# Table reads packed on VectorE, the order of stores and loads on SyncE, and TensorE's set number kept in registers, in the routed stage of a Mamba and mixture-of-experts kernel

## The reference

```
x = x + tanh(g_xattn) * mamba(context, layernorm(x))
h = layernorm(x), 2048 tokens of 512 values
scores = softmax(h @ gate_w.T)                      # 16 experts
weights, ids = top_k(scores, 6), weights normalised to sum 1
out = sum over the six experts e: weight_e * (silu(g) * u) @ w2[e].T, with g, u = split(h @ w13[e].T)   # 352 each
out = out + shared swiglu of width 704, on all tokens
x = x + tanh(g_ffn) * out
```

## Time and profile before

| | |
|---|---|
| median of 3 runs | 1445.77 us (1439.89 to 1447.3) |
| profiled execution | 1442.46 us, span 1440.7 us |
| granted TensorE clock, mean | 0.968 |
| PE, PEld busy | 1321.2 us (92%), 1172.1 us (81%) |
| POOL, DVE, ACT busy | 948.1 us (66%), 853.9 us (59%), 731.9 us (51%) |
| DMA queues q0, q1, q10, share of 16 engines | 23.7%, 23.6%, 7.8% |

### The profile page before, as it was taken

The page is one execution under the profiler, slowest core; times in us unless marked ns, Lnnn a source line. Parts: engine busy times, 40 slices in busy tenths (PEclk is TensorE's granted clock), DMA queues, the critical chain, the costliest instruction groups (busy, mean ns, idle before and its releaser), DMA issues.

```text
span 1440.7 us, 31551 instructions
## 1 busy us (share of the span) xinstructions
PE 1321.2 (92%) x8064; PEld 1172.1 (81%) x8065; DVE 853.9 (59%) x1469; ACT 731.9 (51%) x1317; POOL 948.1 (66%) x671
## 2 busy tenths in 40 slices
PE   7897998998898899999889999999999999999995
PEld 3686887888888799999778878888888888788885
DVE  6878898888999854653344444444444444444442
ACT  5898897898889363333223333333332333333321
POOL 0588899998898657886446645566636665646632
PEclk8899999997999999999999999999999999999998
DMA  4121113221252554564677777888787777877862
GB/s 137 41 72 30 56 64 109 62 99 56 75 166 68 144 123 91 144 151 71 178 174 207 199 212 173 202 208 211 198 182 194 218 195 206 213 183 195 209 165 36
DMA packets 136276, 205.91 MB, mean 143 GB/s; under 512 B 20496, under 2 KB 74384, under 8 KB 134016
## 3 DMA queue, kind: packets, MB, share of 16 engines
q0 software_dynamic: 31024, 62.10, 23.7%
q1 hardware_dynamic: 101744, 102.33, 23.6%
q10 hardware_dynamic: 3440, 40.63, 7.8%
HBM read 130.99 MB, written 76.25 MB: 144 GB/s over the span
## 4 chain that ended last, share of the span: by engine, by line
PE 36%; DMA 14%; issue 7%; DVE 4%; DVEq 4%; POOL 3%; ACT 1%; POOLq 1%; ACTq 0%; SPq 0%
PE bank L1777 11%; PE bank L1757 10%; PE bank L1758 10%; DMA xs<-token_quarters 6%; DMA token_quarters<-xt 4%; DMA xt<-token_rows,gid 3%; PE bank L1768 2%; POOL w L1033 2%; DVEq L1435 2%; DVEq L1429 1%; DVE hs L1223 1%; PE bank L1667 1%; PE bank L1653 1%; ACT ah L908 1%; DVE xl L1423 1%
## 5 line engine op out<-in xcount | busy, mean ns | idle before, releaser
L1757 PE MATMUL bank<-w,xh 128*128 (+1 forms) x1088 | 370.3, 341 | 27.5 <-DVE am L1453 14.7
L995 POOL TENSOR_TENSOR hc<-hs,crow 128x512 f32<-128x512 f32 x254 | 322.0, 1299 | 89.0 <-DVE hs L1223 83.4
L1061 POOL DMA_INDIRECT out_x<-ys,aid x104 | 170.4, 1638 | 277.0 <-issue 234.3
L1758 PE MATMUL bank<-w,xh 128*128 (+1 forms) x1088 | 351.5, 324 | 0.0
L1223 DVE TENSOR_TENSOR_SCAN hs<-dA,bank 128x512 f32<-128x512 f32 x256 | 295.8, 1208 | 50.3 <-PE bank L1667 32.4
L1777 PE MATMUL bank<-w,ah 128*128 (+1 forms) x816 | 262.6, 403 | 20.3 <-DVE al L1459 19.8
L1757 PEld LDWEIGHTS bank<-w,xh 128*128 128x128 f32 x1088 | 204.9, 188 | 60.6 <-issue 56.8
L914 ACT COPY ys<-bank 128x512 f32<-128x512 f32 x136 | 79.8, 586 | 259.6 <-PE bank L1777 259.6
L1758 PEld LDWEIGHTS bank<-w,xh 128*128 128x128 f32 x1088 | 206.9, 190 | 2.3
L1777 PEld LDWEIGHTS bank<-w,ah 128*128 128x128 f32 x816 | 150.5, 190 | 52.5 <-issue 27.2
L1758 PE MATMUL bank<-w,xl 128*128 (+1 forms) x544 | 175.9, 323 | 0.0
(11 more groups left out here) (184 smaller groups left out, 1996.8 us busy)
## 6 DMA issues: line engine op xcount, KB each, us to landing
raws<-in_wall ACTq DMA_DIRECT2D x16, 2176.0 KB, 9.0
token_quarters<-xt SPq DMA_DIRECT2D x104, 256.0 KB, 4.3
xs<-token_quarters SPq DMA_DIRECT2D x104, 256.0 KB, 3.7
crow<-c_rows SPq DMA_DIRECT2D x64, 256.0 KB, 3.2
xt<-token_rows_turned SPq DMA_DIRECT2D x32, 256.0 KB, 3.1
out_x<-ys POOLq DMA_DIRECT2D x32, 256.0 KB, 4.1
token_rows<-rowb SPq DMA_DIRECT2D x4, 1028.0 KB, 6.1
xrow<-in_x SPq DMA_DIRECT2D x4, 1024.0 KB, 8.0
```

The source lines that it names most:

```text
L995: nc.gpsimd.tensor_tensor(hc[:, j, :], hs[:, j, :], crow[:, n % 4, :], ALU.mult).then_inc(hc_done, 1)
L1061: pool.indirect_dma_start(out_rows, bass.IndirectOffsetOnAxis(ap=aid[:, s:s + 1], axis=0), ys[:, s, :], None, bounds_check=TOKENS - 1, oob ...
L1757: nc.tensor.matmul(gate_bank[:, 0:I], xx, columns(w, off + ww + k * 2 * I, I), start=first, stop=last)
L1758: mm = nc.tensor.matmul(up_bank[:, 0:I], xx, columns(w, off + ww + k * 2 * I + I, I), start=first, stop=last)
```

## The change

The unused row 1 of the table now holds three numbers in one word (the next set to prepare, the number of tile t+1's set, and the column of tile t+5), and DVE reads that once a tile and takes it apart by remainder and quotients (`packed` is a new scratch tile for building the word; `sloti` and `odd` go). The ids for the add are copied from `gid` and not from `lists`, for tile t+1 and not t, ahead of `gather_ids`; so they wait for the add of tile t-3. SP stores tile t+1 ahead of the load of tile t (the first store stands ahead of the loop, the last three loads behind it). PE reads the next tile's number in the fourth tile of a round too, and keeps number and offset in two registers over the rounds.

```
@@ -661,10 +660,14 @@
                 for b in range(G):
                     sp.dma_start(gw[b * Q:(b + 1) * Q], gateT[b * P:(b + 1) * P].rearrange("(a c) e -> c a e", c=Q)).then_inc(gw_in, 16)
 
-            def move(t, s, m):
+            def put_quarters(t, s, m=None):
 
                 rows_in(sp, t, s, m, "sp")
+                apart(sp, xt_turned, t - 3, "sp")
                 sp.dma_start(quarters_d[s].rearrange("a p j -> p a j"), xt[:, s, 0:H].rearrange("p (a j) -> p a j", a=G)).then_inc(put[s], 16)
+
+            def set_quarters(t, s, m=None):
+
                 of_slot(sp, put[s], t, m, "sp")
                 apart(sp, xt_turned, t - 3, "sp")
                 sp.dma_start(xs[:, s, :], quarters_d[s].rearrange("a (r g) j -> (a r) (g j)", g=G)).then_inc(moved[s], 16)
@@ -693,10 +696,17 @@
             for t in range(20, NS):
                 x_load(t)
             sp.wait_ge(meta_ready, 2)
-            groups = routed_groups(sp)
-            with sp.Fori(0, groups) as i:
+            looped = sp.value_load(fours[0:1, 2:3], min_val=E // 4 - 2, max_val=ROUTED // 4 - 2)
+            put_quarters(NS, 0)
+            with sp.Fori(0, looped + 1) as i:
                 for k in range(4):
-                    move(4 * i + NS + k, k, i)
+                    put_quarters(4 * i + NS + k + 1, (k + 1) % 4, i + (k + 1) // 4)
+                    set_quarters(4 * i + NS + k, k, i)
+            rest = tiles_but_12(sp) + 8
+            for k in range(3):
+                put_quarters(rest + k + 1, k + 1, looped + 1)
+                set_quarters(rest + k, k, looped + 1)
+            set_quarters(rest + 3, 3, looped + 1)
             tiles = tiles_but_12(sp) + 12
             for s in range(4):
                 apart(sp, added[s], 4 * tiles, "sp")
@@ -1396,9 +1406,6 @@
                 if half == 0:
                     chained(nc.vector.tensor_tensor(slot[:], slot[:], tileno[:, 1, :], ALU.add))
                     chained(nc.vector.tensor_scalar(meta[:, 0, :], slot[:], 1.0, None, ALU.add))
-                    chained(nc.vector.tensor_copy(sloti[:], slot[:]))
-                    chained(nc.vector.tensor_scalar(odd[:], sloti[:], 1, None, ALU.bitwise_and))
-                    chained(nc.vector.tensor_scalar(meta[:, 1, :], odd[:], float(2 * WCOLS), None, ALU.mult))
                     return
                 chained(nc.vector.memset(fresh[:, 0:1], 0.0))
                 chained(nc.vector.tensor_tensor(fresh[:, 1:NT], slot[:, 1:NT], slot[:, 0:NT - 1], ALU.subtract))
@@ -1408,6 +1415,12 @@
                                                        op0=ALU.is_lt, op1=ALU.mult))
                 nc.vector.scalar_tensor_tensor(out=meta[:, 2, :], in0=slot[:], scalar=1.0, in1=fresh[:],
                                                op0=ALU.add, op1=ALU.mult).then_inc(meta_ready, 1)
+                dve.wait_ge(meta_ready, 2)
+                n = NT - AHEAD
+                chained(nc.vector.scalar_tensor_tensor(out=packed[:, 0:n], in0=meta[:, 0, 1:n + 1], scalar=float(NX), in1=meta[:, 2, 0:n],
+                                                       op0=ALU.mult, op1=ALU.add))
+                chained(nc.vector.scalar_tensor_tensor(out=meta[:, 1, 0:n], in0=meta[:, 4, AHEAD:NT], scalar=float(NX * (NX + 1)),
+                                                       in1=packed[:, 0:n], op0=ALU.mult, op1=ALU.add))
 
             def turn(t, s4, m=None):
 
@@ -1422,25 +1435,28 @@
                 source = xt[:, t % 4, 0:H] if isinstance(t, int) and t < NS else banks[4 + 2 * s][:]
                 nc.vector.tensor_tensor(xl[:, s, :], source, xh[:, s, :], ALU.subtract).then_inc(xl_done, 1)
 
-            def take_weight(t, s4, m=None):
-
-                if isinstance(t, int) and t < NS:
-                    return
-                e = dve.value_load(meta[0:1, 0, bass.ds(t, 1)], min_val=1, max_val=NX)
+            def plan_of(t):
+
+                word = dve.value_load(meta[0:1, 1, bass.ds(t, 1)], min_val=0, max_val=NX * (NX + 1) * NR - 1)
+                return dve.snap(word % NX), dve.snap(word // NX % (NX + 1)), dve.snap(word // (NX * (NX + 1)))
+
+            def take_weight(t, s4, number, m=None):
+
                 rows_in(dve, t, s4, m, "dve")
                 at_least(dve, am_done, t - 1)
-                nc.vector.tensor_copy(cc[:, s4 % 2:s4 % 2 + 1], xt[:, s4, bass.ds(H - 1 + e, 1)]).then_inc(cc_done, 1)
+                nc.vector.tensor_copy(cc[:, s4 % 2:s4 % 2 + 1], xt[:, s4, bass.ds(H - 1 + number, 1)]).then_inc(cc_done, 1)
 
             def ids_column(t):
                 return dve.value_load(meta[0:1, 4, bass.ds(t, 1)], min_val=0, max_val=NR - 1)
 
-            def gather_ids(t, s4):
-                nc.vector.tensor_copy(gid[:, s4:s4 + 1], lists[:, bass.ds(ids_column(t), 1)]).then_inc(gid_done, 1)
+            def gather_ids(t, s4, column=None):
+                nc.vector.tensor_copy(gid[:, s4:s4 + 1], lists[:, bass.ds(ids_column(t) if column is None else column, 1)]).then_inc(gid_done, 1)
 
             def add_ids(t, s4):
 
+                apart(dve, gid_done, t + 1, "dve")
                 apart(dve, added[s4], through(t - 4, s4), "dve")
-                nc.vector.tensor_copy(aid[:, s4:s4 + 1], lists[:, bass.ds(ids_column(t), 1)]).then_inc(aid_done, 1)
+                nc.vector.tensor_copy(aid[:, s4:s4 + 1], gid[:, s4:s4 + 1]).then_inc(aid_done, 1)
 
             def multiply(t, s):
                 dve.wait_ge(sg_done, t + 1)
@@ -1468,9 +1484,8 @@
                 if k == EARLY - 1:
                     low.then_inc(wl_done, 1)
 
-            def next_weights(t):
-
-                e = dve.value_load(meta[0:1, 2, bass.ds(t, 1)], min_val=0, max_val=NX - 1)
+            def next_weights(t, e):
+
                 with dve.If(e > 0):
                     apart(dve, raw_in, raws_of(e), "dve")
                     apart(dve, down_done, t, "dve")
@@ -1506,24 +1521,31 @@
                     else:
                         fill_table(i)
 
-            def tile(t, s4, gathers=False, adds=False, m=None):
-                s = s4 % 2
-                if not (isinstance(t, int) and t + 1 < NS):
-                    turn(t + 1, (s4 + 1) % 4, m)
-                a_low(t - 1, 1 - s)
-                take_weight(t + 1, (s4 + 1) % 4, m)
-                if isinstance(t, int):
+            def tile(t, s4, gathers=False, m=None):
+                s, after = s4 % 2, (s4 + 1) % 4
+                if isinstance(t, int) and t < PEELED:
+                    a_low(t - 1, 1 - s)
                     beside(DVE_AFTER_A, t)
-                if isinstance(t, int) and t < NS:
                     for late in FIRST_ROWS.get(t, ()):
                         gather_ids(late, late % 4)
-                elif gathers:
-                    gather_ids(t + AHEAD, (s4 + 1) % 4)
+                    x_low(t + 1, 1 - s)
+                    multiply(t, s)
+                    return
+                split, number, column = plan_of(t)
+                turn(t + 1, after, m)
+                a_low(t - 1, 1 - s)
+                take_weight(t + 1, after, number, m)
+                add_ids(t + 1, after)
+                if gathers:
+                    apart(dve, aid_done, t + 2, "dve")
+                    gather_ids(t + AHEAD, after, column)
+                else:
+                    for late in FIRST_ROWS[t]:
+                        apart(dve, aid_done, t + 2, "dve")
+                        gather_ids(late, late % 4)
                 x_low(t + 1, 1 - s)
-                if adds:
-                    add_ids(t, s4)
                 multiply(t, s)
-
+                next_weights(t, split)
 
             dve.sem_inc(cc_done, NS)
             dve.sem_inc(xt_turned, NS)
@@ -1552,18 +1574,13 @@
             groups = routed_groups(dve)
 
             tile(PEELED, PEELED % 4)
-            next_weights(PEELED)
             for k in range(1, 4):
-                tile(PEELED + k, (PEELED + k) % 4, True, True)
-                next_weights(PEELED + k)
+                tile(PEELED + k, (PEELED + k) % 4, True)
             with dve.Fori(0, groups - 1) as i:
                 for k in range(4):
-                    t = 4 * i + NS + 3 + k
-                    tile(t, (3 + k) % 4, True, True, i + 1)
-                    next_weights(t)
+                    tile(4 * i + NS + 3 + k, (3 + k) % 4, True, i + 1)
             last = tiles_but_12(dve) + 11
             a_low(last - 1, 0)
-            add_ids(last, 3)
             multiply(last, 1)
             a_low(last, 1)
 
@@ -1814,14 +1831,19 @@
                 beside(PE_AFTER_DOWN, t)
             pe.wait_ge(meta_ready, 2)
             groups = routed_groups(pe)
+            carried, carried_old = pe.alloc_register("carried"), pe.alloc_register("carried_old")
+            pe.reg_mov(carried, 2)
+            pe.reg_mov(carried_old, 2 * WCOLS)
             with pe.Fori(0, groups) as i:
-                number = set_number(4 * i + PEELED)
-                old = offset_of(set_number(4 * i + PEELED - 1))
```

(11 more changed lines are left out.)

## The result

| kernel | median us (lowest to highest) | profiled execution, span |
|---|---|---|
| before, beside it | 1446.47 (1439.89 to 1447.3) | 1442.46, 1440.7 |
| after | 1469.16 (1466.95 to 1474.47) | 1467.74, 1466.0 |

The ratio is 1.0172, 95% interval 1.0131 to 1.0214. The change costs some 25 us; the forecast was 8. The direction was right and the size was not.

A forecast was written before the change was run, and what follows sets the result against it. PE was taken as the bound whenever fed. Windows and queueing 14 to 23 us less about 10 outside gave +4 to +13, taken as +8: 1450.5 profiled, 1454 against the median; range 1424 to 1470, the forecast's own 1449 to 1459.

The forecast's parts named there:

- TensorE's registers: PE's table reads at the heads of rounds go; worth 19.7 us where nothing else is late.
- VectorE's table: Three of DVE's four reads go, removing most of 6.8 us `xl` wait; added remainder and quotients cost at most 0.5 us, hidden.
- the ids' wait: DVE's ids copy waits for the add of t-3, delaying tile Q-1 at an expert; nothing added, since Q is later still.
- Outside the windows: The 27 tiles outside the fifteen five-tile windows (Q-4 to Q) give back 12 us, 2.6 only moving a window's start.
- SyncE's order at an expert: Load Q stands behind gather Q+1, the first gather behind the split: windows +14 us, up to +9 for queueing behind a store.
- What a late transpose costs: From DVE's late transpose to the start of its tile on PE: 3.5 us.
- The mechanism forecast: At an expert load Q waits for the delayed gather Q+1, so Q starts late; fifteen windows grow from 522 to 536 us.
- A: Faster rival: load Q lands in 2.6 us, giving 1432; 1407 if gather Q+1's wait did not matter; chance 0.36 with its parts.
- B: Slower rival: load Q served wholly behind the store, 6.0 us instead of 4.1, giving 1482; chance 0.14.
- C: Rival: quotients in registers cost far more than the rows say, deciding from 2 us a tile; chance 0.04.
- Idle ahead of down risen to some 50: Sign at experts: PE idle ahead of "down" rises from 17.6 to some 50 us, DVE's transpose of Q awaiting its load.
- Load Q issued 0.4 us behind store: Sign that the steps are right: at each expert SyncE issues load Q 0.4 us behind store Q+1.

The follow-up runs named there:

- e3: The kernel before with TensorE's carried registers alone: 1425.63 us, ratio 0.9899.
- e4: The kernel before with VectorE's part alone (one packed read, ids copied from `gid` for tile t+1): 1443.28 us, ratio 1.0005.
- e6: The changed kernel with the weights' fetch cut to an eighth, splits reading resident weights, so products are of other weights: 1460.32 us, ratio 1.0121.
- e9: The changed kernel with GpSimd's low split in two halves, one in each of two tiles, the add and gather Q+1 between: 1468.34 us, ratio 1.0185.
- e14: e9 with the weights' fetch in four DMAs, one in each of four tiles, ScalarE carrying the numbers in registers: 1422.24 us, ratio 0.9853.
- e16: e9 with the whole fetch issued at once as two DMAs, in pieces of 1,088 bytes instead of 17,408: 1427.79 us, ratio 0.9868.
- e17: e3 with the whole fetch issued at once as two DMAs in pieces of 1,088 bytes: 1424.66 us, ratio 0.9865.
- e13: e3 with the fetch in four DMAs, one in each of four tiles, and three more table reads on ScalarE per tile: 1551.91 us, ratio 1.0741.
- e5: The changed kernel with SyncE's wait for gather t+1 kept ahead of load t, but store t+1 issued behind that load: 1455.17 us, ratio 1.0074.

## Why the prediction was wrong in size

- **TensorE's registers, 19.7 us: right.** Alone they gave 15 to 18 (e3).
- **VectorE's table: right as to the quotients, wrong as to `xl`.** The three numbers are taken out of the word on the lines that use them, in register operations of 180, 107 and 60 ns at the median (after, L1447, L1453, L1489); before, the two of these lines that had any took 64 and 53 (L1432, L1438). That is 0.23 us more a tile, inside the 0.5 us. But the reads' gain on `xl` was eaten by the ids' wait, to which I had given nothing (e4: 0 us; `xl` wait 14.5 against 6.8). In the changed kernel that error costs nothing: there DVE waits 13.1 us ahead of the ids, none of it for an add, since tile Q-3 is late first. With the fetch out of the way it does cost (e6: DVE waits 46.6 us, PE 26.3).
- **Outside the windows, 12 us less 2.6: right.** Measured 14.3.
- **SyncE's order at an expert, +14 to +23: the step that failed.** It read: "In an even stretch that costs nothing, since the transpose waits long after the landing", and it put the order's whole cost on the load of Q, with the 4 to 5 us seen there. The windows gave +38.5, of which tile Q-3 alone +56.8 and tile Q -15.9. No stall stands ahead of tile Q: Q-1 takes 6.69 us on the mean where it took 6.70. The order took 3.7 us of slack from load Q-2, which is now issued behind the fetch at fifteen experts instead of five, and takes 10 us there. I had the minimum and median of the loads but passed over their maximum, 8.9, though that row was on the page, and no term priced what a load beside a fetch takes: the wait that the sum put at nothing, that of an even stretch, is the one that cost. e9 (no late gather: no change), e14 and e16 (fetch in quarters or short packets: 46 and 40 us less) show it.
- **What a late transpose costs, 3.5 us: too little.** That was read from a short stall. Behind 13 of the 19 stalls PE's clock went to its lower level, and "down" took up to 1.9 us more; some 14 us in all over before.
- **The mechanism forecast exists** (e6: tile Q-1 takes 9.10 us where it took 6.70; the windows are 553.8 instead of the 536 worked out, since the ids' wait is in them too), but in the changed kernel it is behind another stall. I added up costs where the larger hides the smaller, and had the wrong one of the two.
- **Rivals.** A did not come: two windows of fifteen were shorter (39.5 to 37.6 us and 37.1 to 36.9), thirteen longer. The rule of the Trainium skill named there ("DMA: Bandwidth & Descriptors", "Queues, rings and completion order") held, though: in after no load landed before the store issued ahead of it, the nearest 0.40 us behind, while in e5, with the load ahead, the loads landed before the stores. B, a load served wholly behind the store, is right as to the order at load Q-2, whose packets moved behind the store's; its price is not, since the median of the loads in the view is 3.7 us and not 6. C did not come. That 1469.16 lies inside the outer range of 1424 to 1470 is luck: its upper part was B's, and no term of the forecast reached it.
- **What would show it.** "Idle ahead of down risen to some 50": 64.2, but by the transpose of Q-2 and not of Q, so this sign came true for another reason. "Load Q issued 0.4 us behind store": 0.55. "Tiles outside at 6.3 to 6.45": 6.34.

## What to carry to other kernels

Before a transfer is issued later, look at what else the queues carry at its new time and price it with the slowest transfer that the trace shows there (8.9 us here), not the median (3.7); and where several things may be late at one place, take the largest and ask which comes first, since taking away one shows nothing while the other stands. A bulk transfer in rows of 17 KB held the small ones beside it back for as long as it ran. Cutting its rows gave 40 us where a load stood right behind it (e16 against e9), and 1 to 5 us where most did not (e17 against e3). Work on a sequencer between two short instructions of a chain (0.69 us for a read with its branch) cost some 1.2 us a tile in e13 against e3.

## What the runs showed of the hardware that was not expected

- In two stretches beside the fetch two DMA queues moved packets one for one, although these differed 34 and 8.5 times in length: 114 of 17,408 bytes beside 112 of half a KB in 6 us (after), 48 beside 50 of 2 KB in 3 us (e5). At the other experts the small ones got from 0.4 to 1.2 for one (after).
- The same 2.2 MB beside the same loads: a load of 256 KB took up to 10.9 us with the fetch in pieces of 17,408 bytes, 6.6 with 1,088 (e16), 6.8 with 4,352 in four DMAs (e14).
- A load issued 0.55 us behind a store on the same queue never landed before it: the smallest distance was 0.40 us (after).
- A stall of PE of 2.7 us was followed by 3.3 us at a granted clock of 0.55, one of 3.04 us by a clock of 1.00 (after, 1145.3 and 1194.8 us).
